# Attention layer with top-2 experts: raw head outputs packed first, reciprocals spread by GpSimd transfers

## What is computed

```python
q, k, v = (proj(w_q), proj(w_k), proj(w_v))
scores = jnp.einsum('bhqd,bhkd->bhqk', q, k) / jnp.sqrt(jnp.float32(D_K))
attn = jax.nn.softmax(scores, axis=-1)
out = jnp.einsum('bhqk,bhkd->bhqd', attn, v)
out = out.transpose(0, 2, 1, 3).reshape(B, S, HIDDEN)
return jnp.einsum('bse,oe->bso', out, w_o)
...
x = x + _L0_attn_ref(_layernorm(x, axis=-1), ...)
x = x + _L0_ffn_ref(_layernorm(x, axis=-1), ...)
```

## Time and profile before

| | us |
|---|---|
| median of 3 runs | 629.73 |
| lowest, highest | 629.28, 630.07 |
| the profiled execution | 636.47 |
| its span, first to last instruction | 633.7 |
| TensorE busy in it | 584.2 (92%) |
| VectorE busy | 385.4 (61%) |
| ScalarE busy | 329.2 (52%) |
| GpSimd busy | 120.8 (19%) |

### The profile page before, as it was taken

How to read it: one execution, slowest core, us unless ns; L and a number is a source line. 1 busy time by engine, 2 the same in 40 slices (tenths; PEclk the granted TensorE clock), 3 DMA queues, 4 the chain that set the end, 5 groups by cost and what they waited for, 6 DMA issues and landing times.

```text
span 633.7 us, 10494 instructions
## 1 busy us (share of the span) xinstructions
PE 584.2 (92%) x3585; PEld 433.6 (68%) x3585; DVE 385.4 (61%) x689; ACT 329.2 (52%) x481; POOL 120.8 (19%) x137
## 2 busy tenths in 40 slices
PE   2999999999999999999944999999999999998993
PEld 2786673333333333324844999999999999998982
DVE  6715557899999999414456682828364555647140
ACT  5222115777777777661305555647374646565430
POOL 5000111001011010111004004233241507070312
PEclk9899996899999999999755999999999999999897
DMA  8180389257466420135723465655665664843213
GB/s 320 61 99 1 51 110 116 27 77 95 70 94 85 62 87 12 39 123 208 292 104 110 175 244 118 221 162 175 205 167 215 144 251 87 308 75 112 26 13 38
DMA packets 29496, 78.88 MB, mean 124 GB/s; under 512 B 8489, under 2 KB 8745, under 8 KB 24858
## 3 DMA queue, kind: packets, MB, share of 16 engines
q1 hardware_dynamic: 24474, 68.84, 40.6%
q0 software_dynamic: 4992, 9.64, 8.7%
HBM read 58.64 MB, written 9.80 MB: 108 GB/s over the span
## 4 chain that ended last, share of the span: by engine, by line
PE 47%; issue 28%; POOL 9%; DVE 8%; ACT 3%; DMA 2%; POOLq 1%; SPq 0%; ACTq 0%
PE ps_o L592 9%; PE ps L611 7%; PE ps L580 5%; DVE neg_max L1108 5%; PE ps L582 4%; PE ps L581 4%; POOL out L542 4%; PE ps_m L611 3%; PE ps L667 3%; POOL xn L524 3%; PE ps L623 2%; PE ps_o L731 2%; ACT probs_t L936 2%; POOL to_now L537 1%; DMA q_lo<-wq 1%
## 5 line engine op out<-in xcount | busy, mean ns | idle before, releaser
L936 ACT ACTIVATE probs_t<-ps 128x1024 f32<-128x1024 f32 x128 | 123.9, 1023 | 39.5 <-PE ps L623 38.1
L580 PE MATMUL ps<-xgT_hi,w_hi 128*128 128x294 f32 (+1 forms) x416 | 126.9, 305 | 5.3 <-DVE xgT_lo L1284 2.9
L582 PE MATMUL ps<-xgT_hi,w_lo 128*128 128x294 f32 (+1 forms) x416 | 125.8, 303 | 0.0
L581 PE MATMUL ps<-xgT_lo,w_hi 128*128 128x294 f32 (+1 forms) x416 | 125.1, 301 | 0.0
L1108 DVE TENSOR_REDUCE neg_max<-ps 128x1 f32<-128x512 f32 x171 | 111.6, 684 | 11.1 <-PE ps L611 9.0
L1297 DVE TENSOR_TENSOR act<-gate,ps 128x294 f32<-128x294 f32 x48 | 22.0, 461 | 104.6 <-PE ps L582 86.0
L580 PEld LDWEIGHTS ps<-xgT_hi,w_hi 128*128 128x128 f32 (+1 forms) x416 | 78.7, 189 | 5.9 <-DVE xgT_lo L1284 3.2
L581 PEld LDWEIGHTS ps<-xgT_lo,w_hi 128*128 128x128 f32 (+1 forms) x416 | 78.5, 189 | 0.0
L582 PEld LDWEIGHTS ps<-xgT_hi,w_lo 128*128 128x128 f32 (+1 forms) x416 | 78.0, 188 | 0.0
L611 PE MATMUL ps<-k_stack,q_stack 48*128 48x512 f32 x171 | 74.3, 470 | 3.1 <-issue 0.3
L592 PE MATMUL ps_o<-probs_t,v_ones 128*32 128x512 f32 x512 | 70.8, 626 | 0.3 <-ACT probs_t L936 0.3
(11 more groups left out here) (249 smaller groups left out, 959.8 us busy)
## 6 DMA issues: line engine op xcount, KB each, us to landing
w_sb<-w SPq DMA_DIRECT2D x18, 1024.0 KB
w_sb<-w SPq DMA_DIRECT2D x9, 1536.0 KB
w_sb<-w SPq DMA_DIRECT2D x9, 1152.0 KB
q_stack<-q_hi SPq DMA_DIRECT2D x32, 128.0 KB, 5.1
k_stack<-k_hi SPq DMA_DIRECT2D x32, 128.0 KB, 4.8
q_stack<-q_lo SPq DMA_DIRECT2D x16, 128.0 KB, 4.8
k_stack<-k_lo SPq DMA_DIRECT2D x16, 128.0 KB, 5.9
q_hi<-o_norm SPq DMA_DIRECT2D x16, 128.0 KB, 4.0
```

The costliest lines, as they stand in the source:

```text
L580: pe.matmul(o, x_hi, w_hi, start=start, stop=False)
L581: pe.matmul(o, x_hi, w_lo, start=False, stop=False)
L582: return pe.matmul(o, x_lo, w_hi, start=False, stop=stop)
L936: a.activation(probs_t[:, kc % 2, 2 * half:2 * half + 2, :], ps4[:, 2 * (n % 2):2 * (n % 2) + 2, :], ACT.Exp, scale=D ** -0.5).then_inc(s_ ...
```

## The change

The raw output is packed first, and normalised where it is packed. SP packs the even partitions of o_raw into o_all in stage g+1, right behind the transfer of the sums. VectorE's shuffle is gone. GpSimd issues the rest itself: for each group the transfer of the reciprocals to rec_row, which is now 4 partitions x 512, and then four transfers, each of which spreads one head's row over the 16 partitions that this head has in o_all. After the second group of a pair GpSimd multiplies o_all of that pair with rec_all in place, 128 x 512. packed(n) and SP's last wait count these multiplies, one for a pair; ScalarE's copy into o_raw waits for the packing in place of the multiply. rec_row and rec_all change places in memory, o_norm is gone, and the zeroes for the padding rows of the output are read from rec_all.

```diff
--- before.py
+++ after.py
@@ -89,7 +89,7 @@
         k0 = sb(att, "k_stack0", k_shape, f32r)
         v_ones = sb(att, "v_ones", [P, NT, NH, D, 2])
         sum_rec = sb(att, "sum_rec", [P, 2, GH * S // P])
-        rec_row = sb(att, "rec_row", [P, S])
+        rec_all = sb(att, "rec_all", [P, S])
         pro = ExitStack()
         w_hi, w_lo = zip(*((sb(pro, f"w{n}_hi", [P, HC, HID], f32r), sb(pro, f"w{n}_lo", [P, HC, HID], f32r))
                            for n in "qkv"))
@@ -108,8 +108,7 @@
         pro.close()
         probs_t = sb(att, "probs_t", [P, 2, GH, S])
         o_raw = sb(att, "o_raw", [P, 2, S])
-        rec_all = sb(att, "rec_all", [P, S])
-        o_norm = sb(att, "o_norm", [P, 2, S])
+        rec_row = sb(att, "rec_row", [GH, S])
         att.close()
         proj.close()
 
@@ -211,7 +210,7 @@
         s_so = [sem(f"s_so{r}") for r in range(2)]
         s_rc = sem("s_rc")
         s_rb = sem("s_rb")
-        s_sh = sem("s_sh")
+        s_sh = [sem(f"s_sh{r}") for r in range(2)]
         s_on = sem("s_on")
         s_oc = [sem(f"s_oc{r}") for r in range(2)]
         s_zero, s_zt = sem("s_zero"), sem("s_zt")
@@ -335,8 +334,8 @@
 
             sp.wait_ge(s_zero, 3)
             for m in range(SUBS):
-                sp.dma_start(out[T + m * P:T + (m + 1) * P, :], rec_row[:, :]).then_inc(s_init, 16)
-            sp.dma_start(xn2_dram[0:1, :], rec_row[0:1, :]).then_inc(s_rows, 16)
+                sp.dma_start(out[T + m * P:T + (m + 1) * P, :], rec_all[:, :]).then_inc(s_init, 16)
+            sp.dma_start(xn2_dram[0:1, :], rec_all[0:1, :]).then_inc(s_rows, 16)
 
             def ready(pair):
 
@@ -366,18 +365,14 @@
                         sp.dma_start(qs[(g // 2) % RING][row:row + 1, 2 * (g % 2):2 * (g % 2) + 2, :].bitcast(f32)
                                      .rearrange("a p (t c) -> a (p t) c", c=P),
                                      max_rows[8 * par:8 * par + 8, g % 2, :].bitcast(f32)).then_inc(s_row[g % 4], 16)
-                g = s - 2
-                if 0 <= g < NG:
-                    sp.wait_ge(s_rc, g + 1)
-                    if g >= 1:
-                        sp.wait_ge(s_sh, g)
-                    sp.dma_start(rec_row[1:P:2 * D, :], sum_rec[:, g % 2, :]).then_inc(s_rb, 16)
                 g = s - 1
                 if 0 <= g < NG:
                     sp.wait_ge(s_or, g + 1)
                     if g >= 2:
                         sp.wait_ge(s_rb, 16 * (g - 1))
                     sp.dma_start(sum_rec[:, g % 2, :], o_raw[1:P:2 * D, g % 2, :]).then_inc(s_so[g % 2], 16)
+                    sp.dma_start(o_all[64 * (g % 2):64 * (g % 2) + 64, g // 2, :],
+                                 o_raw[0:P:2, g % 2, :]).then_inc(s_oc[g % 2], 16)
                 if s in (-4, -3) or s >= 2:
                     pair = (s + 4) // 2 if s < 0 else (s + 6) // 2
                     if pair < NG // 2:
@@ -395,12 +390,7 @@
                     stack(1, range(2), "k")
                     ready(2)
                     stack(2, range(2), "qk")
-                g = s - 2
-                if g >= 0:
-                    sp.wait_ge(s_on, g + 1)
-                    sp.dma_start(o_all[64 * (g % 2):64 * (g % 2) + 64, g // 2, :],
-                                 o_norm[0:P:2, g % 2, :]).then_inc(s_oc[g % 2], 16)
-                if g == 8:
+                if s == 10:
                     sp.dma_start(wo_sb, wo.rearrange("p (c e) -> p c e", c=HC)).then_inc(s_wo, 16)
                     sp.dma_start(gw_sb[:, :, :], gw.rearrange("p (c e) -> p c e", c=HC)).then_inc(s_gw, 16)
                 if s in (NG - 2, NG - 1):
@@ -409,7 +399,7 @@
                     sp.dma_start(x1[:, b * TPB:(b + 1) * TPB, :], x_t[:, b * TPB:(b + 1) * TPB, :]).then_inc(s_x[b], 16)
 
             sp.wait_ge(s_pv, TPB * NG)
-            sp.wait_ge(s_on, NG)
+            sp.wait_ge(s_on, NG // 2)
 
 
 
@@ -469,7 +459,7 @@
         def _(pool):
             pool.memset(ident[:, :], 0.0).then_inc(s_zero, 1)
             pool.memset(before_b[:, :], 1.0).then_inc(s_zero, 1)
-            pool.memset(rec_row[:, :], 0.0).then_inc(s_zero, 1)
+            pool.memset(rec_all[:, :], 0.0).then_inc(s_zero, 1)
             pool.wait_ge(s_zero, 3)
             pool.affine_select(out=ident[:, :], in_=ident[:, :], compare_op=ALU.not_equal, fill=1.0,
                                base=0, pattern=[[-1, P]], channel_multiplier=1).then_inc(s_const, 1)
@@ -509,12 +499,26 @@
             pool.wait_ge(s_job, len(jobs))
             prepare(3)
 
-            for g in range(NG):
-                pool.wait_ge(s_sh, g + 1)
-                if g >= 2:
-                    pool.wait_ge(s_oc[g % 2], 16 * (g // 2))
-                pool.tensor_tensor(o_norm[:, g % 2, :], o_raw[:, g % 2, :], rec_all[:, :],
-                                   ALU.mult).then_inc(s_on, 1)
+            pool.wait_ge(s_init, 16 * SUBS)
+            pool.wait_ge(s_rows, 16)
+            for pair in range(NG // 2):
+                for r in range(2):
+                    g = 2 * pair + r
+                    pool.wait_ge(s_rc, g + 1)
+                    if g >= 1:
+                        pool.wait_ge(s_sh[(g - 1) % 2], 16 * GH * ((g - 1) // 2 + 1))
+                    pool.dma_start(rec_row[:, :], sum_rec[:, r, :]).then_inc(s_rb, 16)
+                    pool.wait_ge(s_rb, 16 * (g + 1))
+                    if pair >= 1:
+                        pool.wait_ge(s_on, pair)
+                    for j in range(GH):
+                        at = 64 * r + D * j
+                        pool.dma_start(rec_all[at:at + D, :],
+                                       rec_row[j:j + 1, :].unsqueeze(1).broadcast_to([1, D, S])).then_inc(s_sh[r], 16)
+                for r in range(2):
+                    pool.wait_ge(s_oc[r], 16 * (pair + 1))
+                    pool.wait_ge(s_sh[r], 16 * GH * (pair + 1))
+                pool.tensor_tensor(o_all[:, pair, :], o_all[:, pair, :], rec_all[:, :], ALU.mult).then_inc(s_on, 1)
             pool.wait_ge(s_pv, TPB * NG)
             pool.memset(w2_sb[:, FC - 1, :], 0.0).then_inc(s_tail, 1)
 
@@ -670,8 +674,7 @@
 
             def packed(n):
 
-                for r in range(2):
-                    pe.wait_ge(s_oc[r], 16 * n // 2)
+                pe.wait_ge(s_on, n // 2)
 
             def projection(t):
 
@@ -924,7 +927,7 @@
                         a.wait_ge(s_pv, TPB * (g + 1))
                         if g >= 2:
                             a.wait_ge(s_so[g % 2], 16 * (g // 2))
-                            a.wait_ge(s_on, g - 1)
+                            a.wait_ge(s_oc[g % 2], 16 * (g // 2))
                         a.activation(o_raw[:, g % 2, :], ps_o[:, :], ACT.Copy).then_inc(s_or, 1)
                     if 0 <= s < NG:
                         n = s * UNITS + u
@@ -1149,11 +1152,6 @@
                         v.reciprocal(sum_rec[:, g % 2, :], sum_rec[:, g % 2, :]).then_inc(s_rc, 1)
                         if s in (NG - 1, NG):
                             residual(s - (NG - 1))
-                    if u2 == 11 and g >= 0:
-                        v.wait_ge(s_rb, 16 * (g + 1))
-                        if g >= 1:
-                            v.wait_ge(s_on, g)
-                        v.stream_shuffle(rec_all[:, :], rec_row[:, :], [1] * 32).then_inc(s_sh, 1)
 
             for b in range(B):
                 for t in range(b * TPB, (b + 1) * TPB):
```

## The result

The changed kernel took 648.64 us (646.48 to 654.83, 4 runs), against 629.90 us for the kernel before (629.28 to 633.22, 4 runs). The ratio is 1.0291, 95% interval 1.0251 to 1.0331. The likeliest time given was 625.4 us and the range ended at 641. The time went to the other side, by the mechanism of rival A at a price of c = 12.2, and with the shared reading of rival B in it.

What follows compares the result with a forecast made beforehand. VectorE and TensorE were taken to pace each other in attention's stages. Removing the shuffle gave 3.8 us over 11 stages plus 0.5 us, 4.3 us off 629.73: 625.4 us, range 624 to 641 us, with other terms covered.

Steps and rivals of the forecast that it cites:

- rival A: GpSimd's serial chain for a group outlasts the stage: from c = 10.75, 16 c - 172.0 us on top; chance 0.32.
- c: GpSimd's cycle per group, transfers, landings and half a multiply: forecast 10.1 us, bounds 5.9 and 15.3, against a stage of 11.00.
- rival B: Broadcasts read one partition one after another, 2.8 us each: c about 17 us, time near 725 us; chance 0.04.
- The shuffle's price: VectorE in attention: 0.345 us in each of 11 stages plus 0.5 us in stage 13, together 4.3 us.
- The stage of 11.00 us: Attention stage without a shuffle, from 115.38: taken as the new pace, instead of 11.345 us.
- The early packing at nothing: SP's queue: packing ahead of the stacking transfers costs 0 us, covered by some 10 us of stage.
- The route by which the loss comes: Sign of being wrong: SP waits for rec_row before the sums, VectorE for sum_rec, TensorE for max rows; or a tail gap.
- the limit c = 10.75: Tail block: with a backlog, the last multiply's end meets TensorE's need of the last pair, 297.6, at this cycle.
- the formula of rival A: Price of GpSimd's backlog: 16 c - 172.0 us on top of 625.4 us.
- the sum for c: GpSimd per group: 3.1 first transfer, 3.3 issues, 2.9 last landing, 0.64 half a multiply, 0.2 waits: 10.1 us.
- Rivals C and D: C: another pacer holds 11.3 us, 629 to 630 us, 0.05; D: VectorE blocks GpSimd's descriptor writing, near 661 us, 0.02.
- the near side: The forecast case, GpSimd's cycle within its limit: 624 to 628 us, chance 0.57.

Runs made afterwards that it cites:

- e1: Kernel before with only VectorE's shuffle left out, so the normalisation isn't done: 628.53 us, ratio 0.9946 to the kernel before.
- e7: Kernel before with only the early packing and one multiply a pair in o_all; shuffle and SP's transfers stay: 633.20 us, ratio 1.0019 to before.
- e8: Changed kernel with one broadcast transfer a group in place of four, and rec_row's rows in partitions 0, 4, 8, 12: 626.81 us, ratio 0.9935 to before.
- e3: Changed kernel with two rec_row buffers, GpSimd waiting for broadcasts only at the multiply or buffer reuse: 628.51 us, ratio 0.9950 to before.
- e2: Changed kernel with each broadcast reading 16 partitions of k_hi instead of one row of rec_row: 626.28 us, ratio 0.9914 to before.

## Why the prediction was wrong

**What held.** The shuffle's price: 4.3 us forecast, 3.9 us at the end of the projections in e1, 3.4 us in its median (1.4 to 5.4). The stage of 11.00 us: it appears in the changed kernel for as long as GpSimd's lag is under a stage. The early packing at nothing: e7, 1.0019. The route by which the loss comes (SP's wait for rec_row, the sums, VectorE, the tail block) is in the trace; the limit c = 10.75 itself no run tries. By the formula of rival A, c = 12.2 gives 625.4 + 195.2 - 172.0 = 648.6 us. (The formula adds 0.64 us at the end; with that counted c is 12.14, and the time 647.7.) The agreement with 648.64 is closer than the formula deserves, and luck in part: the formula knows no clock, while in the trace some 8 us come as longer stages, in part at a lower clock, and the rest as gaps and again a lower clock in the tail.

**The step that failed is the sum for c.** Its largest error is the landing of the last broadcast, put at 2.9 us. Its terms, and their means in the timeline of GpSimd, for the last group with nothing else running, for the two halves, and for all groups (us; the measured terms hold all waits):

| term | forecast | last group | groups 0 to 7 | groups 8 to 15 | all 16 |
|---|---|---|---|---|---|
| issue to landing of rec_row, with the wait | 3.1 | 2.6 | 5.1 | 2.6 | 3.8 |
| three further issues | 3.3 | 1.5 | 1.5 | 1.5 | 1.5 |
| landing of the last broadcast, with the wait | 2.9 | 4.9 | 6.6 | 6.0 | 6.3 |
| half a multiply | 0.64 | 0.64 | 0.64 | 0.64 | 0.64 |
| other waits | 0.2 | - | - | - | - |
| cycle | 10.1 | 9.7 | 13.7 | 10.7 | 12.2 |

With nothing else running, two errors cancelled, by luck. The issues were put at more than twice their length (1.1 us, measured 0.49), since I took the gathers' 98 rows as the nearest thing. The last landing was put 2 us too short, since it took 128 KB out of one path as if they came out of many. The single group is even a little quicker than forecast. The mean is not, since the landings were priced with empty engines: the DMA share of 0.6 in the earlier trace rows was named under rival A, but had no term in the sum. Over all groups the two landings are 4.1 us over the forecast and the issues 1.8 us under it.

The lag is built by groups 1 to 7, up to 234 us. There the first transfer takes 4.4 to 7.4 us up to the first broadcast, and the cycles are 15.8, 12.1, 12.2, 13.6, 15.5, 14.4 and 14.7 us. The stacking transfers run until about 218 us. Part of the load is the change's own: SP is released by the landing of rec_row and issues the next packing (128 KB) beside the broadcasts, and the packing's median landing goes from 4.0 us before to 6.3 us. The issues by line, first of the kernel before and then of the changed one (KB, median us to landing):

```profile
q_hi<-o_norm SPq DMA_DIRECT2D x16, 128.0 KB, 4.0
```

```profile
q_hi<-o_raw SPq DMA_DIRECT2D x16, 128.0 KB, 6.3
...
rec_row<-sum_rec POOLq DMA_DIRECT2D x16, 8.0 KB, 2.4
```

A slow first transfer alone does not keep a lag: in e8 it takes 4.1 to 6.0 us in groups 1 to 8 too, and a lag of 5.3 us at group 3 is gone by group 10. The broadcasts there land sooner. How the 2.3 us between 9.9 us, the mean of the last two groups, and 12.2 us divide among stacking and packing was not tried.

**Rival B** was priced by a packet's usual time, served one by one, 2.8 us a broadcast. The runs give 1.15 us, from a shared path and not from one partition. Its sign is in the trace: in the last group the landings, each from its own issue, grow from 3.2 over 3.9 and 4.6 to 4.8 us. It was given 0.04 because "nothing in the trace shows such queueing"; the trace of before has no large transfer that reads few partitions, so it could not have shown it. The packing and the stacking read 64 partitions each, and the transfer of the sums reads four but only 8 KB.

**Rivals C and D** didn't occur: the maxima ran at 11.00 us beside the transfers, and the issues took 0.48 to 0.63 us beside them, so VectorE's maxima didn't hold the descriptors up. On that the trace agrees with the rule of the Trainium skill that the prediction cites (SBUF — State Buffer, "Who interferes with whom"). The longest of these issues, 0.63 us at 302.48, stood beside one of VectorE's four normalisations; whether it was held up by it is not shown, and it costs 0.14 us.

**The chances.** c was 0.65 us under its limit with terms that could each be off by a microsecond, and every 0.1 us above it cost 1.6 us. 0.57 for the near side was too much, and the upper end of 641 us stood at c = 11.7, so that a cycle 20% over the sum was already outside.

## What to carry to other kernels

When a small tile is the source of a broadcast by DMA, place its rows in different groups of four partitions: here 0, 4, 8, 12 instead of 0, 1, 2, 3 turned a loss of 2.9% into a gain of 0.6%. Other placings than these and 0, 32, 64, 96 weren't run. A chain of transfers that one queue waits out in order is to be priced with the landings of the busiest stage, and compared with the stage's length before anything else. Where it comes near, take the landings out of the chain with a second buffer, as in e3.

## What the runs showed of the hardware

- Partitions 0 to 3 together deliver 25 to 28 GB/s to the DMA engines, be they four or sixteen: 128 KB in 4.6 us with sixteen engines and in 5.2 us with four, but 1.4 us with four engines when the rows are four partitions apart.
- A direct transfer on GpSimd's queue costs 0.49 us of issue for 16 rows of 2 KB, 0.60 us for 64, and 0.73 us for 128 runs of 64 bytes. In the last case, with nothing else running, it lands after 2.3 us; SP's lands about 1.8 us after its issue starts.
- TensorE's granted clock in nearly the same code behind the projections differs between the profiled executions. The stretch from the end of the projections to the weights' conversion takes 30.2 us before, 29.6 us in e3 and 24.5 us in e2. Some 10 us of it, in e3 and in e2 (the number behind POOL's count is the clock):

```profile
306.60:316.50 9.90, 9.47 (x46) 9.37 (x44) 0.39 (x6) 3.67 (x5) 0.00 (x0) 0.50 0.99 371
```

```profile
307.20:317.00 9.80, 5.08 (x55) 4.79 (x53) 4.41 (x38) 3.00 (x6) 0.00 (x0) 0.70 0.91 341
```

In e3 TensorE works through this stretch at 0.50, that is 1.2 GHz; in e2 it is through with its matmuls after some 5 us. It had been busy ahead of it in both, but for 0.28 us in e3; the kernel before had no such gap and was at 0.50 from 312 to 322 us as well. That accounts for the 4 to 5 us between the spans of e3 and e2. The spread of 8 us among the runs of one kernel goes with the clock too: runs of the kernel before with a mean clock of 0.949 have spans of 633.0 to 634.0 us, those with 0.962 or 0.963 of 627.5 to 628.7 us. What decides it these runs don't show.
